# Splitting eight PSUM banks four and four, not five and three, between attention scores and projections

## The reference

```python
xn = adaln(x, cond, ln1)                 # layer norm, scale and shift from cond
q, k, v = split(xn @ qkv_w.T);  q, k = rope(q), rope(k)
x = x + attn(q, k, v) @ sa_out_w.T       # softmax over 256 keys, 16 heads
xn = adaln(x, cond, ln2)
q = rope(xn @ q_w.T);  k = rope(ctx @ k_w.T);  v = ctx @ v_w.T
x = x + attn(q, k, v) @ ca_out_w.T       # ctx: another 16 x 256 x 512 input
xn = adaln(x, cond, ln3)
x = x + gelu(xn @ ffn_w1.T + b1) @ ffn_w2.T + b2      # 2048 hidden channels
```

## Time and profile before

| | us |
|---|---|
| median of 3 executions (1893.96 to 1896.38) | 1894.43 |
| the profiled execution | 1894.98 |
| its span, first to last instruction | 1892.9 |
| PE busy | 1856.1 (98%) |
| PEld busy | 1621.5 (86%) |
| ACT busy | 1428.4 (75%) |
| DVE busy | 1284.7 (68%) |
| POOL busy | 801.5 (42%) |

### The profile page before, as it was taken

One profiled execution on the slowest core, in us unless ns is written; L12 is line 12 of the kernel. 1 busy time (PEld: TensorE's weight loads), 2 busy tenths in 40 slices (PEclk: granted clock), 3 DMA queues, 4 the chain that ended last, 5 costly groups with the idle time before them and its releaser, 6 DMA issues. The chain is left out here.

```text
span 1892.9 us, 38411 instructions
## 1 busy us (share of the span) xinstructions
PE 1856.1 (98%) x13460; PEld 1621.5 (86%) x13460; DVE 1284.7 (68%) x2241; ACT 1428.4 (75%) x3811; POOL 801.5 (42%) x834
## 2 busy tenths in 40 slices
PE   8899999999999999999999998999999999999999
PEld 7788888888878888988988987788898888989898
DVE  6877667777777776776776776346766676666754
ACT  5788888888888898888888899555656566666654
POOL 3534433433443554544544554104535445353531
PEclk9999999999999999999999999999999999999999
DMA  7677766676687677677677687433131323223130
GB/s 226 204 212 207 218 206 205 193 209 184 190 234 216 195 237 226 191 222 224 190 226 220 192 239 184 130 113 122 57 112 57 113 77 94 96 73 107 45 101 34
DMA packets 307375, 311.46 MB, mean 165 GB/s; under 512 B 22000, under 2 KB 259952, under 8 KB 307184
## 3 DMA queue, kind: packets, MB, share of 16 engines
q1 hardware_dynamic: 306576, 308.67, 55.0%
q10 hardware_dynamic: 608, 0.34, 0.1%
HBM read 212.46 MB, written 92.27 MB: 161 GB/s over the span
## 5 line engine op out<-in xcount | busy, mean ns | idle before, releaser
L780 ACT ACTIVATE ps_s<-ps_s,neg_max 128x256 f32<-128x256 f32 x1024 | 461.8, 454 | 50.6 <-DVE neg_max L895 47.6
L895 DVE TENSOR_REDUCE neg_max<-ps_s 128x2 f32<-128x512 f32 x512 | 348.9, 686 | 196.4 <-PE ps_s L651 196.0
L794 ACT ACTIVATE prob<-ps_s 128x512 f32<-128x512 f32 x512 | 308.2, 603 | 84.9 <-PE ps_s L672 81.4
L976 POOL TENSOR_TENSOR rope_c<-rope_c,rope_s 128x256 f32<-128x256 f32 x128 | 98.5, 770 | 312.1 <-DVE rope_s L870 312.1
L651 PE MATMUL ps_s<-kT,qT 96*128 96x256 f32 x1024 | 218.7, 296 | 10.1 <-ACT ps_s L780 6.7
L672 PE MATMUL ps_s<-qT,kT 112*128 112x256 f32 x1024 | 209.1, 286 | 9.9 <-ACT ps_s L780 9.1
L780 ACT ACTIVATION_READ_ACCUMULATOR ps_s<-ps_s,neg_max 128x1 f32 x1024 | 218.1, 213 | 0.0
L651 PEld LDWEIGHTS ps_s<-kT,qT 96*128 96x128 f32 x1024 | 167.8, 189 | 57.0 <-ACT ps_s L780 24.5
L641 PE MATMUL ps_g<-xx_hi,w_hi 128*128 128x256 f32 x1024 | 206.0, 283 | 2.0 <-issue 1.4
L641 PE MATMUL ps_g<-xx_hi,w_lo 128*128 128x256 f32 x1024 | 203.4, 280 | 0.0
L1347 PE MATMUL ps_y<-w_hi,h_hi 128*128 128x512 f32 x512 | 201.8, 394 | 0.3
(11 more groups left out here) (157 smaller groups left out, 4701.1 us busy)
## 6 DMA issues: line engine op xcount, KB each, us to landing
kT<-k_turned SPq DMA_DIRECT2D x384, 128.0 KB, 3.1
qT<-q_turned SPq DMA_DIRECT2D x128, 256.0 KB, 3.8
f_raw<-in_w1T SPq DMA_DIRECT2D x124, 256.0 KB, 2.9
k_turned<-rot_hi SPq DMA_DIRECT2D x64, 256.0 KB, 3.1
k_turned<-rot_lo SPq DMA_DIRECT2D x64, 256.0 KB, 2.5
q_turned<-rot_hi SPq DMA_DIRECT2D x64, 256.0 KB, 3.8
q_turned<-rot_lo SPq DMA_DIRECT2D x64, 256.0 KB, 4.1
qT<-q_turned SPq DMA_DIRECT2D x128, 128.0 KB, 4.0
```

The lines of the kernel that those rows point to most:

```text
L780: ins = eng.activation(scores[:, t * L:(t + 1) * L], scores[:, t * L:(t + 1) * L], ACT.Exp, bias=neg_max[G % 2][:, t, j:j + 1], accum_out= ...
L794: eng.activation(prob[:, n % NP, :, :].rearrange("p t l -> p (t l)"), ps_s[:, score_bank(step), :], ACT.Exp).then_inc(exp_done, 1)
L895: eng.tensor_reduce(neg_max[G % 2][:, :, j], ps_s[:, score_bank(step), :].rearrange("p (t l) -> p t l", l=L), AX.X, ALU.max, negate=True). ...
L976: eng.tensor_tensor(rope_c[n % 2][:, 0, :], rope_c[n % 2][:, 0, :], rope_s[:, 0, :], ALU.subtract)
```

## The change

The ring `ps_g` gets a fourth bank and the ring `ps_s` loses its fifth. Nothing else is touched: the list of steps, every instruction and every transfer stay as they are; only the bank that each user writes and the release that it waits for change.

```diff
@@ -336,11 +336,11 @@
         elif (step[0] == "project" and step[4] == 0) or step[0] in ("mod", "mod_turn", "early"):
             bank_users.append(step)
     bank_turn = {step: n for n, step in enumerate(bank_users)}
-    NB = 3
+    NB = 4
 
     score_users = [step for step in order if step[0] in ("scores", "weigh", "max_turn", "mix")]
     score_turn = {step: n for n, step in enumerate(score_users)}
-    NS = 5
+    NS = 4
```

## The result

The changed kernel takes 1946.5 us (median of four, 1944.6 to 1950.3) against 1894.2 for the old one: 1.0276 times as long, with a 95% interval of 1.0258 to 1.0294, 52 us more. The forecast was 1953, "slower".

A forecast was written before the change was run, and what follows sets the result against it. PE's own instruction list was taken to bound the attention stage. Terms 30 + 12 + 6 + 7 + 5 + 1 - 2 = 59 us on 1894.4 gave 1953 us; the walk's range was 1935 to 1975 (0.62), the wider one 1915 to 1995.

The forecast's parts named there:

- What bounds the kernel: Attention stage: PE's own instruction list sets its end; PE busy 446.97 of 450 us and 469.05 of 470.
- The fourth projection bank: Prologue: it removes only waits of `ps_g` users, mainly for `rope_s`; 2 us gained, bounds 0 and 7.
- The walk of the first layer: From 100 to 550 us: delays followed through one item, 2.4 us each over 12.5 items, 30 us lost.
- The walk of the second layer: From 640 to 1110 us: waits at `weigh 319`, `weigh 326`, `mix 40`, 0.88 us an item, 12 us lost.
- The rest: Irregular stretches: 6 us lost from 550 to 640, 7 from 1110 to 1190, 5 before 100, 1 after 1190.
- Shared delay: Attention items: ACT's queue decides, so an item loses only its largest shortage, 0.9 or 0.3 us; 1920 us, chance 0.17.
- All shortages add up: Score ring: every release moves with PE, 110 us lost, 2004 us; chance 0.15 together with the clock rival.
- the lower bound: Score ring: shortages within ten microseconds are one delay, 41 us in 43 clusters, less absorption: 20 us.
- The clock: Attention stage: longer PE waits bring half-clock stretches, 44 us on top, 1997 us; chance 0.15 together with summed shortages.
- Projection bank pays more: Prologue: the projection bank gains more than the score bank costs, at most 7 us, 1887 us; chance 0.03.
- nothing changes: Whole kernel: PE's waits absorb the shortages, time within 0.2% (4 us); chance 0.03.
- What should have shown: Profile signs: L780 waits before L651 and L672 from 36 to some 80 us; items of 38.3 and 36.3 us.

The follow-up runs named there:

- seven banks: Changed kernel with three projection banks in place of four, score banks still four, one of eight banks idle: 1946.6 us, ratio 1.0269.
- the rest first: Changed kernel with `o_low` (the rest of a mix, on DVE) moved before the turn of x it stood behind: 1931.8 us, ratio 1.0190.
- the scaling later: Changed kernel with DVE's two scalings of x for an item ahead 8 places later in the first layer: 1941.5 us, ratio 1.0249.
- both moves: Changed kernel with `o_low` before the turn of x and DVE's scaling of x 8 places later: 1929.5 us, ratio 1.0183.

## Why the prediction was right, and where its terms were off

**What bounds the kernel.** Right. PE's list sets the end: the end of the attention stage moved from 1211.9 to 1267.6 us in the profiled executions, 55.7, and the span by 55.3.

**The fourth projection bank.** I took 2 us of gain. The waits for `rope_s` went, but with seven banks, where 3.0 us of them are back, the time is the same (0.1 us by the medians). So this term was worth nothing that the runs can tell: PE came to the next wait earlier, for `w_lo`. It lies inside the bounds of 0 to 7.

**The walk of the first layer.** Forecast 2.4 us an item, measured 2.36. Step by step, as weight loads of the two traces laid beside each other give it: `max_turn 19` +0.86 (0.86 forecast); `scores 163` takes back 0.70 (0.50); `weigh 150` then +1.28 to 1.44 over the item's start (1.44); 0.13 is given back at the projection right after it. I had 0.12 from `weigh 152`, where nothing was given back (1.32 us behind before it and after it): that the two are of one size is luck. `weigh 154` +1.03 (1.02). The 12 items from head 32 to head 224 lost 28.5 us; the forecast had 30 for 12.5. That the last part is a delay of its own, and not covered by the others, is shown by the run with the rest first; that the first part comes from DVE's queue is shown for 1.08 of its 1.32 us, by the run with the scaling later.

**The walk of the second layer.** Forecast 0.88, measured 0.61: this term was mis-sized. `weigh 319` +0.39 and `weigh 326` +0.27 were right. But each wait was followed by a refund, 0.07 after the first (as forecast) and 0.14 after the second (not forecast), and the mix added 0.17, not 0.29: its release followed PE only in part. Over the 13.3 items that is 8 us in place of 12.

**The rest.** From head 224 to 256, 6.5 us (forecast 6 for the stretch); from head 464 to the last, 5.9 (7 + 1); up to head 32, 4.2 (5 - 2). With 28.5 for the first layer and 8.3 for the second that makes 53.4 us; the late transfer, 2.0 us, is no part of the change. The medians say 52, the forecast 59. The second layer came out 4 us below its term, the end 2 and the first layer 1.5, and the prologue 1 above, as the 2 us of the projection bank did not come.

**The rivals.** *Shared delay* (1920) fell: an item would have lost 0.9, and "both moves" shows two delays that add up. *All shortages add up* (2004) fell too: `scores 165` and `mix 18` cost nothing. Both its 110 us and the 20 of the lower bound subtract present waits, and these hold the 11.9 us behind the mixes that are no waits for a bank; the walk of the items does not use them. *The clock* had a small part. PE's granted clock was halved in 17 us of the changed kernel's attention stage against 10 before, by the clock's record. Two of the four falls, each with the stretch ahead of it (columns as in the earlier trace rows):

```profile
47.40:50.80 3.40, 0.34 (x3) 0.37 (x4) 2.68 (x5) 1.02 (x4) 0.06 (x1) 1.00 1.11 305
50.90:57.60 6.70, 5.41 (x26) 5.12 (x25) 6.40 (x13) 3.62 (x14) 4.08 (x6) 0.50 0.87 214
589.50:593.50 4.00, 1.97 (x11) 1.37 (x10) 3.48 (x4) 2.23 (x7) 3.02 (x4) 1.00 0.69 211
593.60:597.00 3.40, 3.40 (x11) 2.84 (x10) 0.69 (x1) 3.35 (x9) 3.16 (x3) 0.50 0.92 241
```

Ahead of the four falls PE was busy for 0.34 of 3.4, 1.97 of 4.0, 1.74 of 3.5 and 1.82 of 3.4 us; none came in the regular items, whose waits of 1.3 us left the clock whole (1.00 from 100 to 550 us). The section of the Trainium skill that the prediction cites ("TensorE: Matmul & The Clock Gate", section "A second HAM failure mode: psum-queue depth-cycling") speaks of cycling through PSUM banks, not of few of them, and the swing that it describes did not come in the regular items. The 6.8 us more at half the clock cost at most 3.4 us of the 52, which sit in the terms above already. *Projection bank pays more* and *nothing changes*: the first falls with the run with seven banks, the second with the result.

**What should have shown.** "From 36 to some 80 us" for the waits of `scores` and `weigh` on L780 was wrong: they are 41.0. All waits for L780 and `o_lo` together are 82.9, so the 80 fits only the sum over all users. The 36 was read wrongly too. It took 11.9 us behind the mixes for waits for a bank, so that the waits that are one grew from 24.1 to 41.0. The 38.3 us of a first-layer item were right, the 36.3 of a second-layer one were 36.08.

## What to carry to other kernels

To price a buffer fewer, set the start of every user against the release of the user that many places before it, and then walk one period: a wait moves the releases that depend on PE and not those already in a queue, and a wait that was there takes some of it back. Neither the sum of the shortages (110 us) nor their largest per burst (20) was near the 52 us.

A name beside idle time is the last release that the profile finds, and not always the cause. Before you count idle time as a wait for a buffer, set it against the end of that release: 28 of 51 "waits" here had a bank that was long free, and they stayed in every run.

Count what the odd users of a ring hold. Four banks for the alternating pair alone cost 0.22 us an item, four with two odd users for every eight heads 2.36. Where an edit only shortens one engine's queue, see what is late next: the scaling moved 8 places took a wait away and made another, in another ring.

## What the runs showed of the hardware

- **A wait is partly paid back.** After a wait PE's weight loads come closer for a moment: in the old item `weigh 150` at 412.58 was followed by its projection at 412.93 by the timeline, 0.35 us later; after the wait, 437.18 and 437.41 above, 0.23 later. The old trace has this in the shape of a longer load (0.43 for the two, against 0.30). It was worth 0.13 us after `weigh 150`, 0.14 after `weigh 358` and 0.07 after `weigh 351`, and nothing after `weigh 154`; what decides that is not shown. I had counted on the 0.07 alone.
- **Weight loads run ahead of narrow matmuls.** The 32 loads of a mix take 1.45 us from 399.79, its 32 matmuls 1.93; then the loads stand still for 0.41 us. No run had less there, whatever its rings.
- **Tiny DVE instructions of 1 us.** The three that make and split the shift work on 16 columns each. In more than half of the groups each takes 0.17 us; in the others two of them take up to 1.27 and 1.02 us. The old kernel, DVE, in one group:

```profile
408.10 0.70 DVE L903 TENSOR_TENSOR shift<-neg_max,log_sb 128x16 f32<-128x16 f32 x1
408.83 0.17 DVE L905 TENSOR_REDUCE max_parts<-shift 128x16 fp32r<-128x16 f32 x1
409.04 1.02 DVE L908 TENSOR_TENSOR max_parts<-shift,max_parts 128x16 f32<-128x16 f32 x1
...
426.51 0.17 DVE L908 TENSOR_TENSOR max_parts<-shift,max_parts 128x16 f32<-128x16 f32 x1
```

  and POOL at the same time:

```profile
407.85 0.92 POOL L977 TENSOR_TENSOR rope_c<-rope_c,rope_s 128x256 f32<-128x256 f32 x1
408.73 1.30 POOL L983 TENSOR_TENSOR rot_lo<-rope_c,rot_hi 128x512 fp32r<-128x512 f32 x1
```

  L903 starts while L977 runs and ends at 408.80, 0.03 after it; L908 ends at 410.06, 0.03 after L983. In the other group POOL is idle then. All 64 groups of this trace agree: wherever L903 or L908 takes more than 0.3 us (27 times each), a POOL instruction runs and ends 0.03 us before it, and in the 35 and 36 groups in which POOL is idle they take at most 0.18. The reduction between them, with one input, takes 0.17 us in all 64, beside POOL or not. So these instructions of DVE with two SBUF inputs are held until POOL's is over. The Trainium skill ("SBUF — State Buffer", section "SBUF: two separate sides") describes this: DVE and GpSimd share a pair of ports, and whichever starts first has it for its whole instruction; the rows agree. These 1.4 us lie in the very queue that makes `max_turn` late. No run moved POOL's instructions away, so what that would save is open.
